# A graph layer on one core: four node pairs added by VectorE at the seam, w_r issued by ScalarE, the second weight copy loaded in parts, rank steps moved into the edge tiles, a reordered tail

## What is computed

```python
agg  = segment_sum(x[src], dst)          # x: 50000 x 512 f32, 62500 edges sorted by dst
deg  = segment_sum(ones, dst)
mean = agg / max(deg, 1)[:, None]
h    = mean @ W_l + b + x @ W_r          # both 512 x 512
y    = x + h * sigmoid(h)
out  = layernorm(y)                      # over the 512 columns, eps 1e-5
```

## Time and profile before

| | |
|---|---|
| median of 3 runs | 1562.06 us (1561.3 to 1563.25) |
| profiled execution | 1561.28 us, its span 1559.5 us |
| TensorE matmul busy | 1517.1 us (97%) |
| VectorE busy | 1322.9 us (85%) |
| ScalarE busy | 1184.5 us (76%) |
| POOL busy | 1008.4 us (65%) |
| DMA mean | 255 GB/s; 276 GB/s in the node pairs |
| chain that ended last | TensorE 90%, VectorE 3%, ScalarE 2%, DMA 2% |

### The profile page before, as it was taken

How to read it: one execution, slowest core, us unless ns; L and a number is a source line. 1 busy time by engine, 2 the same in 40 slices (tenths; PEclk the granted TensorE clock), 3 DMA queues, 4 the chain that set the end, 5 groups by cost and what they waited for, 6 DMA issues and landing times.

```text
span 1559.5 us, 23957 instructions
## 1 busy us (share of the span) xinstructions
PE 1517.1 (97%) x7198; PEld 1244.9 (80%) x7198; DVE 1322.9 (85%) x2088; ACT 1184.5 (76%) x1609; POOL 1008.4 (65%) x1097
## 2 busy tenths in 40 slices
PE   7799999999999899999999999999999999999996
PEld 6688778888887788888888888888888888888884
DVE  7699999999998788888878888888888888888886
ACT  4354333333334799999989999999999999999996
POOL 6466556666662767766757767767667676676673
PEclk9999999999999999999999999999999999999998
DMA  5655588888887689999999999899999999999995
GB/s 191 172 178 188 170 243 266 263 257 271 262 266 231 185 263 286 273 274 278 269 267 286 275 278 271 275 274 277 270 288 268 283 272 276 274 277 267 283 267 182
DMA packets 298965, 397.68 MB, mean 255 GB/s; under 512 B 42652, under 2 KB 144822, under 8 KB 298837
## 3 DMA queue, kind: packets, MB, share of 16 engines
q1 hardware_dynamic: 250855, 321.43, 68.8%
q0 software_dynamic: 46944, 74.22, 17.5%
q10 hardware_dynamic: 1038, 0.50, 0.1%
HBM read 335.97 MB, written 139.67 MB: 305 GB/s over the span
## 4 chain that ended last, share of the span: by engine, by line
PE 90%; DVE 3%; ACT 2%; DMA 2%; issue 2%; SPq 0%; POOL 0%; POOLq 0%; DVEq 0%; ACTq 0%
PE pH L530 81%; PE pT L634 5%; PE pT L603 3%; PE pT L541 1%; DMA cor<-correction_rows,node_idx 1%; ACT O L805 1%; DMA light_x<-in_x 1%; DVE Z L905 1%; ACT cor L751 0%; DVE cor L896 0%; DMA wr_raw<-in_L_gnn_W_r 0%; DVE w_sum L900 0%; DVE Z L900 0%; ACT pH L817 0%; DVE w_sum L905 0%
## 5 line engine op out<-in xcount | busy, mean ns | idle before, releaser
L442 POOL DMA_INDIRECT cor<-correction_rows,node_idx x347 | 395.6, 1140 | 259.2 <-ACT cor L751 186.0
L530 PE MATMUL pH<-ws_hi,x_hi 128*128 128x512 f32 x876 | 348.7, 398 | 6.6 <-ACT pH L817 4.2
L530 PE MATMUL pH<-ws_hi,x_lo 128*128 128x512 f32 x876 | 343.9, 393 | 0.0
L530 PE MATMUL pH<-ws_lo,x_hi 128*128 128x512 f32 x876 | 343.6, 392 | 0.0
L530 PE MATMUL pH<-wb_hi,x_hi 128*128 128x512 f32 x688 | 280.1, 407 | 0.0
L530 PE MATMUL pH<-wb_hi,x_lo 128*128 128x512 f32 x688 | 273.1, 397 | 0.0
L530 PE MATMUL pH<-wb_lo,x_hi 128*128 128x512 f32 x688 | 272.9, 397 | 0.0
L805 ACT ACTIVATE O<-Z,shift,rstd 128x512 f32<-128x512 f32 x347 | 262.4, 806 | 3.6 <-DVE shift L1128 3.6
L1118 DVE BATCH_NORM_STATS2 stats<-Z 128x6 f32<-128x512 f32 x347 | 219.4, 673 | 0.3 <-issue 0.3
L1110 DVE TENSOR_TENSOR Z<-Z,X 128x1024 f32<-128x1024 f32 x174 | 211.3, 1215 | 2.9 <-ACT Z L829 2.9
L829 ACT ACTIVATE Z<-pH 128x1024 f32<-128x1024 f32 (+1 forms) x172 | 175.2, 1019 | 48.5 <-PE pH L530 48.2
(11 more groups left out here) (148 smaller groups left out, 2767.9 us busy)
## 6 DMA issues: line engine op xcount, KB each, us to landing
X<-in_x SPq DMA_DIRECT2D x173, 512.0 KB, 4.5
out<-O SPq DMA_DIRECT2D x173, 512.0 KB, 4.8
xs<-in_x SPq DMA_DIRECT2D x344, 128.0 KB
correction_rows<-c_out SPq DMA_DIRECT2D x98, 256.0 KB, 4.1
light_x<-in_x SPq DMA_DIRECT2D x58, 256.0 KB, 2.8
light_h<-early_product SPq DMA_DIRECT2D x44, 256.0 KB
out<-light_o SPq DMA_DIRECT2D x44, 256.0 KB, 4.1
join_row<-joined SPq DMA_DIRECT2D x98, 64.0 KB, 4.0
```

The costliest lines, as they stand in the source:

```text
L442: g.indirect_dma_start(out=out_, out_offset=None, in_=table, in_offset=bass.IndirectOffsetOnAxis(ap=idx, axis=0), bounds_check=bound, oob_ ...
L530: last = mm(ps, a[:, k], w[:, k], start=(n == 0 and not onto), stop=(n == len(terms) - 1), skip_group_check=onto)
```

## The change

- ScalarE's queue issues the four w_r transfers, ahead of the edge lists; SP issues w_l alone.
- The eight parts of the second weight copy are issued one behind each of the tiles 8 to 15; POOL's sums go from tiles 14 to 17 to tiles 18 to 21, ScalarE's rounding from 18 to 20 on, POOL's splits from 20 to 25 on.
- Six of nine `loop_cols` passes stay ahead of the edge tiles; the others come at edge tiles 12, 26 and 40, `mark_rows_before` at 46 instead of 4, `find_nodes` at 54 instead of 6. TensorE no longer waits for `rdeg_ready` there. ScalarE keeps early tile 42 ahead of the first `round_sums`.
- The resets before the seam are spread: the light one at edge tile 89, the first three pairs' at 90, 91 and 92 (all at 93 before).
- Four pairs (ADDED) instead of two are added by VectorE and not seeded. For the first pairs ScalarE rounds the next x ahead of silu. POOL gathers the corrections of pairs 0 and 1 before those of the first light tile.
- Light tiles take four pairs each for the first 39 and three pairs each for the last five (`lights`), so that nothing of them stands behind the last pair. In the tail ScalarE takes the last silu first, and VectorE makes the shift of pair 172 before the moments of pair 173.

```diff
@@ -32,8 +32,10 @@
-    assert EARLY - 1 == NP // 4
+    HURRIED = 5
+    assert 4 * (EARLY - HURRIED) + 3 * (HURRIED + 1) <= NP
     LATE = 28
+    ADDED = 4
@@ -224,10 +226,17 @@
-        def light_tail(light, first, end):
-
-            for k in range(first, end):
-                light(k // 4, k % 4)
+        def lights(light, t):
+            every_fourth = 4 * (EARLY - HURRIED)
+            if t < every_fourth:
+                light(t // 4, t % 4)
+            else:
+                l, s = divmod(t - every_fourth, 3)
+                l += EARLY - HURRIED
+                if l <= EARLY:
+                    if s == 0:
+                        light(l, 0)
+                    light(l, s + 1)
@@ -274,7 +283,6 @@
                 sp.dma_start(wl_raw[:, k], w_l[k * P:(k + 1) * P, :]).then_inc(weights_in[k], 16)
-                sp.dma_start(wr_raw[:, k], w_r[k * P:(k + 1) * P, :]).then_inc(weights_in[k], 16)
@@ -294,11 +302,13 @@
             sp.wait_ge(wl_split, K)
-            for w, tile in ((w_l, wb_raw), (w_r, xs)):
-                for i in range(4):
-                    sp.dma_start(tile[32 * i:32 * i + 32], w[i * P:(i + 1) * P].rearrange("(k a) n -> a k n", a=32)
-                                 ).then_inc(wb_in, 16)
-            peeled(8, EARLY - 8, move_early)
+            for n in range(8):
+                single(8 + n, move_early)
+                w, tile = (w_l, wb_raw) if n < 4 else (w_r, xs)
+                i = n % 4
+                sp.dma_start(tile[32 * i:32 * i + 32], w[i * P:(i + 1) * P].rearrange("(k a) n -> a k n", a=32)
+                             ).then_inc(wb_in, 16)
+            peeled(16, EARLY - 8, move_early)
@@ -376,12 +386,10 @@
                 shifted(t, q, u, -3, NP, store_out)
-                light(q, u)
+                lights(light, t)
             peeled(0, NP, move)
-            light_tail(light, NP, 4 * EARLY)
...
                 single(t, store_out)
-            light_tail(light, 4 * EARLY, 4 * EARLY + 4)
@@ -420,17 +428,17 @@
                 single(4 + k, split_early)
-            peeled(8, 14, split_early)
+            peeled(8, 18, split_early)
...
                 g.tensor_tensor(wb_raw[:, k], wb_raw[:, k], xs[:, k], ALU.add).then_inc(wb_summed, 1)
-                single(14 + k, split_early)
-            peeled(18, 20, split_early)
+                single(18 + k, split_early)
+            peeled(22, 25, split_early)
...
                 g.tensor_tensor(wb_lo[:, k], wb_raw[:, k], wb_hi[:, k].bitcast(f32), ALU.subtract).then_inc(wb_split, 1)
-                single(20 + k, split_early)
-            peeled(24, 4 * FIND_ROUND, split_early)
+                single(25 + k, split_early)
+            peeled(29, 4 * FIND_ROUND, split_early)
@@ -486,6 +494,14 @@
+            def light_first(q, u):
+                if u == 0:
+                    light_at(q - 1, light_make_rstd)
+
+            def light_last(q, u):
+                if u == 2:
+                    light_at(q + 1, gather_light)
@@ -498,22 +514,19 @@
-            gather_light(0)
...
             single(1, gather_cor)
+            gather_light(0)
...
             def serve(t, q, u):
-                if u == 0:
-                    light_at(q - 1, light_make_rstd)
+                lights(light_first, t)
...
                 shifted(t, q, u, 3, NP, gather_cor)
-                if u == 2:
-                    light_at(q + 1, gather_light)
+                lights(light_last, t)
...
             single(NP - 1, make_rstd)
-            light_make_rstd(EARLY - 1)
@@ -612,7 +625,6 @@
             def mark_rows_before():
-                pe.wait_ge(rdeg_ready, 1)
@@ -644,7 +656,7 @@
                 three(pH[b][:, 0, :], s_hi[b], s_lo[b], wl_hi, wl_lo).then_inc(c_product, 1)
-                if t == 4:
+                if t == 46:
@@ -660,12 +672,14 @@
                     pe.wait_ge(c_made, ET - 1 + t)
+                elif t < ADDED:
+                    pe.wait_ge(z_made, t - 1)
                 else:
-                    pe.wait_ge(seeded, t - 1)
+                    pe.wait_ge(seeded, t - ADDED + 1)
...
                     last = three(pH[b][0:rows, a, :], x_hi[b][:, :, a, 0:rows], x_lo[b][:, :, a, 0:rows],
-                                 w_hi, w_lo, onto=t >= 2)
+                                 w_hi, w_lo, onto=t >= ADDED)
@@ -673,6 +687,8 @@
             a_ = nc.scalar.activation
+            for k in range(K):
+                act.dma_start(wr_raw[:, k], w_r[k * P:(k + 1) * P, :]).then_inc(weights_in[k], 16)
@@ -710,13 +726,13 @@
             peeled(1, 8, early_tile)
-            peeled(8, 4 * MERGE_ROUND + 2, early_tile)
+            peeled(8, 4 * MERGE_ROUND + 4, early_tile)
...
                 a_(wb_hi[:, k], wb_raw[:, k], ACT.Copy).then_inc(wb_rounded, 1)
-                single(4 * MERGE_ROUND + 2 + k, early_tile)
-            peeled(4 * MERGE_ROUND + 2 + K, EARLY - 4, early_tile)
+                single(4 * MERGE_ROUND + 4 + k, early_tile)
+            peeled(4 * MERGE_ROUND + 4 + K, EARLY - 4, early_tile)
@@ -745,9 +761,10 @@
-                if t == 4 or t == 5:
-                    act.wait_ge(z_made, t - 3)
-                wait(act, seeded, t - 5)
+                if t - 4 < ADDED:
+                    wait(act, z_made, t - 3)
+                else:
+                    act.wait_ge(seeded, t - 4 - ADDED + 1)
@@ -761,8 +778,8 @@
             single(0, carry)
+            single(EARLY - 2, keep_early)
             single(0, round_sums)
-            single(EARLY - 2, keep_early)
@@ -773,12 +790,11 @@
                 shifted(t, q, u, 3, ET, expand_mask)
-                if fixed(t) and t == ET - 5:
+                if t == ET - 9:
...
                     reset_light(0)
-                    single(0, reset_cor)
-                    single(1, reset_cor)
-                    single(2, reset_cor)
+                if ET - 8 <= t < ET - 5:
+                    single(t - (ET - 8), reset_cor)
@@ -809,7 +825,10 @@
                 b, used = ring(q, u, 4)
-                wait(act, silu_made, t - 1)
+                if t - 2 < ADDED:
+                    act.wait_ge(z_made, t - 1)
+                else:
+                    act.wait_ge(silu_made, t - 1)
@@ -819,7 +838,7 @@
                 b = u % 4
-                if t < 2:
+                if t < ADDED:
@@ -847,20 +866,22 @@
             def node_pair(t, q, u):
-                shifted(t, q, u, -1, NP, silu)
-                shifted(t, q, u, 1, NP, round_x)
-                if t >= 1:
+                if t <= ADDED:
+                    shifted(t, q, u, 1, NP, round_x)
+                    shifted(t, q, u, -1, NP, silu)
+                else:
+                    shifted(t, q, u, -1, NP, silu)
+                    shifted(t, q, u, 1, NP, round_x)
+                if t + 1 >= ADDED:
...
                 shifted(t, q, u, 3, NP, reset_cor)
-                light(q, u)
+                lights(light, t)
...
             peeled(0, NP, node_pair)
+            single(NP - 1, silu)
             single(NP - 3, normalise)
-            single(NP - 1, silu)
             single(NP - 2, normalise)
-            light_tail(light, NP, 4 * EARLY)
             single(NP - 1, normalise)
-            light_tail(light, 4 * EARLY, 4 * EARLY + 4)
@@ -1054,21 +1075,23 @@
             then(v.tensor_copy(loop_col[0], pH[1][:, 0]))
-            loop_cols(0, col_bits - 2)
+            loop_cols(0, col_bits - 3)
...
             single(2, subtract)
-            loop_cols(col_bits - 2, col_bits - 1)
             single(0, split_sums)
-            loop_cols(col_bits - 1, col_bits)
-            v.memset(upto[:, 0:1], 0.0)
-            v.tensor_copy(upto[:, 1:1 + NTILES], loop_col[col_bits % 2][:, 0:NTILES]).then_inc(upto_ready, 1)
...
                 shifted(t, q, u, 1, ET, split_sums)
-                if t == 6:
+                if t in (12, 26, 40):
+                    n = col_bits - 3 + (t - 12) // 14
+                    loop_cols(n, n + 1)
+                if t == 40:
+                    v.memset(upto[:, 0:1], 0.0)
+                    v.tensor_copy(upto[:, 1:1 + NTILES], loop_col[col_bits % 2][:, 0:NTILES]).then_inc(upto_ready, 1)
+                if t == 54:
@@ -1166,23 +1189,21 @@
             def node_pair(t, q, u):
-                if t == 1 or t == 2:
+                if 1 <= t <= ADDED:
...
                 shifted(t, q, u, -2, NP, make_shift)
-                light(q, u)
+                lights(light, t)
...
             single(NP - 1, residual)
+            single(NP - 2, make_shift)
             single(NP - 1, moments)
-            single(NP - 2, make_shift)
-            light_tail(light, NP, 4 * EARLY)
             single(NP - 1, make_shift)
-            light_tail(light, 4 * EARLY, 4 * EARLY + 4)
```

## The result

The changed kernel took 1559.51 us in the median (1557.19 to 1562.31, 20 runs) beside 1562.99 us of the kernel before (1560.38 to 1567.98, 20 runs): ratio 0.9976, 95% interval 0.9968 to 0.9984. It is faster by 0.24%, some 3.5 us, where 19.0 were forecast; 1543 and the whole range 1536 to 1551 are missed. The profiled execution took 1558.54 us (span 1556.7), 2.7 less than the one of before.

A forecast was written before the change was run, and what follows sets the result against it. TensorE was taken to bound the kernel, with some 42 us of its idle time and slow matmuls to be had. The terms summed to 19.0 us off the profiled 1561.28, giving 1542.3 and a median of 1543 us; range 1536 to 1551.

The forecast's parts named there:

- Lights: Last light tiles in three pairs instead of four: -0.3 us for more ACT work and transfers, bounds 0 and -3.
- Seam: First node pairs: with four pairs added by DVE, pair 2 no longer waits for its seed, +5.8 us, bounds +2 and +6.1.
- Rival D: Seam wait reappears at pair 4 for its seed: 4 us of 5.8 gone, 1547; counted inside the forecast's 0.68.
- Second copy, one part per tile: Early tiles: spreading the eight weight parts removes the stop at 50 us, +9.4 us, bounds +9.9 and +6.
- Rival C: Early tiles: each weight part holds up a load, eight stops, 38 us instead of 9.9: 1580; chance 0.04.
- POOL's sums: Early tiles 18 to 21: four POOL sums lengthen DVE's column passes before the hand-over, -4.1 us, bounds -6.5 and 0.
- Hand-over: From early to edge tiles: fewer passes before the scan, no gap or slow restart, +6.6 us, bounds +3.5 and +6.6.
- Ranks and finding the nodes: Edge tiles: three rank passes are not hidden, find_nodes only moves, -5.1 us, bounds -3.5 and -10.
- rival A: Three edge-stage stops and the wait for the found rows each end with a slow-clock restart, 8 us: 1551; chance 0.14.
- rival B: DVE's edge-stage inserts are cheap (-3.5 instead of -5.1) and the merge-to-hand-over chain is shorter: 1538; chance 0.10.
- Resets, start, tail: Resets spread before the pairs +1.6 us; w_r issued by ACT at the start +1.3; shorter end after the last matmul +3.8.
- buys nothing net: Whole kernel: the terms at their worse bounds at once, so no net gain; chance 0.04.

The follow-up runs named there:

- e2: The changed kernel, with the third and fourth light steps sharing a pair instead of the first and second in the last five light tiles; 1548.54 us, ratio 0.9911.
- e1: The changed kernel with one light tile per four pairs up to the end and the old tail back; 1551.9 us, ratio 0.9936.
- e9: The changed kernel with the edits of e5 and e6 together; 1551.6 us, ratio 0.9928.
- e13: e10 with the second copy's sums on DVE, its parts issued with tiles 5 to 12, and DVE's shift of pairs 0 to 2 moved; 1544.97 us.
- e7: e2 without POOL's four sums of the second weight copy; 1549.61 us, ratio 0.9915.
- e10: e2 with the mask row of edge tile 4 loaded ahead of the wait for the last early products; 1549.02 us, ratio 0.9915.
- e3: The changed kernel with all nine rank passes back ahead of the edge tiles, mark at edge tile 4, find_nodes at 6; 1557.98 us, ratio 0.9974.
- e4: The changed kernel with two pairs added by VectorE instead of four; 1558.67 us, ratio 0.9978.
- e6: The changed kernel with SP issuing the next light tile's load one pair earlier in the hurried part; 1558.62 us, ratio 0.9972.
- e5: The changed kernel with ScalarE alone doing its hurried light steps as (0), (1, 2), (3); 1561.41 us, ratio 0.9993.

## Why the prediction was wrong

**What bounds the kernel.** Right: TensorE's idle time and slow matmuls were the only thing to win, and no stage got faster within itself, but for 0.6 us in the pairs. Incomplete: I asked which stops go, and only once what a stage that never stood can lose.

**Lights: the step that failed.** "The price is six lights in three pairs each instead of four: ACT ... 0.15 us of 5.97, the transfers 5% more" priced the amount, -0.3. The amount costs at most 0.7 us (e2). The step grouping put ScalarE's normalise into the pair in which DVE makes its shift, and DVE's addition one pair behind its load. That was readable in the new function: it runs two steps in the first pair of a light. From pair 159 to 170 it cost 7.8 us, of which e1 and e2 lose nothing and e9 0.6; to the last matmul it is 8.0. My bound of -3 was no bound, since it covered only more work and no new wait. This is 7.7 of the 15.5 us that miss.

**Seam: mis-sized, +5.8 forecast, +1.9 measured.** The mechanism was right, pair 2 starts without its wait. I had DVE's splits 0.6 and 0.5 us ahead and 0.2 late by adding durations, without DVE's waits for POOL's rstd (0.93, 0.93, 0.60). With them pairs 4 and 5 stop for 0.69 and 1.32 us, and 3.3 of 5.2 us go back by pair 20. e13 gets 1.6 back by moving that wait. The forecast's own check ("none over 0.5 us in pairs 2 to 6") would have told it. Rival D had the sign of this, the wait moving, and nearly its size (4 of 5.8 us gone, measured 3.9), but the wrong wait: seed(4) was in time.

**Second copy, one part per tile.** +9.4 forecast, +9.5 to tile 10, and then 2.4 lost by tile 16; in sum 7.1, inside the bounds of +6 and +9.9. The trace's landing times of the tile loads beside the parts are 2.7 us at least, 3.4 in the median and 5.1 at most; the last one is the stop of 1.66 us at 63 us. It is my own sign of being wrong, a load that lands 4 us after issue, and it came once. Eleven other profiles with the parts in the same places lose 0.4 to 1.2 us between tiles 10 and 16, so "0.5 in all" was near, and most of the 2.4 belongs to this one execution. Rival C's eight stops did not come.

**POOL's sums.** -4.1 forecast, -4.4 measured, and e7 shows that they are the cause: without them 36.23 us from tile 28 to 38, with them 40.13 in e2. The wait for the found rows was 1.21 us (2.4 forecast). Two predicated copies take 3.45 us with POOL beside both and 2.48 beside one. The Trainium skill, "SBUF — State Buffer", "Who interferes with whom", says that a VectorE instruction with two inputs in SBUF contends with a GpSimd instruction that reads SBUF; this case agrees, about 1 us for each. The mask that the prediction shows for this rule has one such input, and is lengthened as much: the rule for two inputs does not cover it.

**Hand-over.** +6.6 forecast, +6.4 measured (6.2 to 6.4 in every profile that spreads the passes); the first edge group takes 3.05 us instead of 5.46 at clock 1.00. The working has a slip: 1.3 + 0.65 + 0.7 is 2.65 and not 2.75; measured are 2.77 from scan to matmul. What I missed is next in line: the mask row that SP issues behind the landing of the last store, 0.8 us here, which the slow start of the edge stage had hidden (e10).

**Ranks and finding the nodes.** -5.1 forecast, -5.5 measured (1.86, 1.77, 1.88), idle 1.20, 1.12 and 1.24, no slow restart behind them: rival A's clock is refuted here, rival B too. find_nodes moved without cost as said, though it costs 1.4 us in each place, not 1.17, and its mark, which I left out, 1.3 more. e3 prices the other side: with the passes ahead of the scan the hand-over wins 0 instead of 6.4. So moving them won 6.4 and paid back 5.5: 0.9 net, where 1.5 were forecast, and the 0.8 lost to the mask row takes nearly all of it.

**Resets, start, tail.** +1.2 of 1.6; the gap in front of the pairs fell from 1.01 to 0.19 us. Start +0.6 against +1.3, inside its bounds: DVE's second sum began at 8.94 instead of 9.33 but took 1.18 us beside POOL instead of 0.69, so the first weight matmul came at 10.87, 0.1 later than before and not near 9.5. ScalarE's copy of the first tile came 1.8 us later, much as I had priced it (1.5, "still in time"), and with it POOL's split, from 6.53 to 8.30, beside this sum. The 0.6 was won only behind it. By the rule of the Trainium skill named in the prediction ("Issuing engines are not separate DMA queues") it would be 0.5, my estimate from one issue; the one profile with w_r back on SP says 1.6. The size stays open. Tail +3.5 of 3.8; 11.5 us from the end of the last matmul instead of 15.0, and 10.8 in e2, where nothing is late ahead of it.

**The sum.** Forecast 19.0, measured 3.5 by the medians. The difference is 7.7 lights, 3.9 seam, 2.3 late loads, 0.8 mask row, 0.7 start and 0.4 or less each for resets, passes, sums, hand-over and tail, against 0.6 won in the pairs, and 0.7 by which the medians and the profiled executions differ. The biggest are waits that took the place of removed ones or were newly made; none is an instruction that I had the wrong length for. Of these terms the hand-over and the resets come out alike in the other profiles, and the lights within 1 us (8.8 from pair 159 to 170 in e3 and e4); the start, the late loads, the column passes, edge tiles 1 to 4 and the seam vary by 1 us and more from one to the next. The time of 1559.5 lies above A's range too (1548 to 1556): only "buys nothing net", at 0.04, was near it, and A's mechanism, the clock, was not the one.

## What to carry to other kernels

When steps are regrouped in a software pipeline, list for each step which engine's step of the same round it now waits for; here it cost 7.8 us in a stage where TensorE had never stood, and an average load ("0.15 us of 5.97") says nothing of it. When taking away one of two waits changes little or nothing, take away both before dropping the theory. Where a stage starts earlier, go through what its first transfers are queued behind: the old delay had hidden one here. And when work is moved out of a gap, price the gap and the new place as one sum.

## What the runs showed that was not expected

- A TensorE stop of 1.1 to 1.2 us cost 1.8 to 1.9 us of starts; the granted clock stayed 1.00 over the edge stage in spite of three of them.
- In e7 TensorE idled 2.70 us at 175.95, and from the fifth matmul of the next group on they took 0.59 to 0.63 us instead of 0.39 to 0.40, for about 3 us, then 0.39 again: the granted clock was 0.50 there (the 1.2 GHz level). After 2.03 us idle at 179.35 in e6 it stayed 1.00; in the kernel before, after 2.23 and 1.28, it was 0.50 from 177 to 182.
- Single profiles of kernels with equal code in a stretch differ by up to 1.3 us in pairs 1 to 3 and by 1.1 us at the start, as much as some of the terms forecast here. Over the whole way to pair 156 four kernels with equal code (the changed one, e1, e5, e6) were 7.2, 10.7, 4.1 and 6.3 us ahead of the kernel before.
- VectorE's wait of 1.9 to 3.3 us ("remote" in three of four kernels) ahead of the second edge output came in some kernels and not in others with the same code there; it stays unexplained.
